# Shared expert tile moved to the end of the first expert pass, and a shorter start of the attention loop

## The reference

```
x = x + 0.5 * ffn(layernorm(x))      # first expert pass
x = x + attention(layernorm(x))      # 16 query heads, 4 key/value groups, head size 16, causal
x = x + 0.5 * ffn(layernorm(x))      # second expert pass, same weights
```

## Time and profile before

| | |
|---|---|
| median of 3 runs | 416.62 us (414.96 to 417.93) |
| profiled execution | 416.29 us, of which 414.5 us span |
| busy share | PE 90%, DVE 59%, ACT 35%, POOL 42% |
| first expert pass ends (last scatter issued) | 126.06 us |
| first scores of the loop | 170.67 us |
| step 3 of the loop | 185.66 us |
| last scatter of the second pass issued | 404.58 us |

### The profile page before, as it was taken

How to read it: one execution, slowest core, us unless ns; L and a number is a source line. 1 busy time by engine, 2 the same in 40 slices (tenths; PEclk the granted TensorE clock), 3 DMA queues, 4 the chain that set the end, 5 groups by cost and what they waited for, 6 DMA issues and landing times.

```text
span 414.5 us, 8450 instructions
## 1 busy us (share of the span) xinstructions
PE 374.9 (90%) x3164; PEld 294.5 (71%) x3171; DVE 243.0 (59%) x732; ACT 143.7 (35%) x296; POOL 175.3 (42%) x288
## 2 busy tenths in 40 slices
PE   8999999999998698888999999998699999999980
PEld 6769999999673455555566665555399999989660
DVE  5889852222222647778878778889757874222220
ACT  3221111111110234565767657577334111111110
POOL 1041425552111254556767664565812215643111
PEclk9999999999999979999999999999989999999996
DMA  8959932299103524202213042200211101398000
GB/s 266 409 207 351 333 106 76 66 334 333 40 16 114 156 81 126 56 20 78 78 48 105 20 121 71 55 28 28 59 57 37 43 25 56 103 345 318 27 23 14
DMA packets 27055, 50.04 MB, mean 121 GB/s; under 512 B 4458, under 2 KB 20590, under 8 KB 25975
## 3 DMA queue, kind: packets, MB, share of 16 engines
q1 hardware_dynamic: 19118, 25.10, 18.7%
q0 software_dynamic: 4512, 21.50, 15.1%
q10 hardware_dynamic: 3376, 2.80, 2.3%
HBM read 35.16 MB, written 6.55 MB: 101 GB/s over the span
## 4 chain that ended last, share of the span: by engine, by line
PE 67%; DVE 17%; DMA 5%; issue 4%; SPq 3%; ACT 1%; another core or an unknown queue 1%; POOL 1%; POOLq 0%; DVEq 0%; ACTq 0%
PE bank L1003 25%; PE bank L1024 13%; PE bank L1228 3%; PE bank L1457 3%; PE bank L1485 3%; PE bank L1386 2%; PE bank L542 2%; DVE mxa L1416 2%; PE bank L993 2%; PE bank L965 2%; PE bank L1514 2%; SPq L1333 1%; PE bank L1379 1%; DVE area L1534 1%; PE bank L592 1%
## 5 line engine op out<-in xcount | busy, mean ns | idle before, releaser
L1003 PEld LDWEIGHTS bank<-area,W 128*128 128x128 f32 x1024 | 119.9, 193 | 3.5 <-ACT area L1093 1.7
L1003 PE MATMUL bank<-area,W 128*128 128x128 f32 x1024 | 120.9, 277 | 1.2 <-ACT area L1093 1.2
L1172 DVE TENSOR_TENSOR area<-area,bank 128x512 f32<-128x512 f32 x34 | 23.4, 687 | 71.5 <-issue 49.7
L1464 ACT ACTIVATE area<-bank 128x512 f32<-128x512 f32 x96 | 54.2, 597 | 27.8 <-PE bank L1457 27.4
L1024 PE MATMUL bank<-W,area 128*128 128x256 f32 x256 | 60.9, 381 | 1.8 <-DVE area L1157 1.8
L1473 POOL TENSOR_SCALAR_AFFINE_SELECT area<-area 128x512 f32<-128x512 f32 x64 | 40.8, 650 | 40.5 <-ACT area L1464 40.2
L1104 ACT ACTIVATE area<-bank 128x512 f32<-128x512 f32 x34 | 20.3, 597 | 97.1 <-PE bank L1003 87.5
L1024 PEld LDWEIGHTS bank<-W,area 128*128 128x128 f32 x256 | 46.2, 190 | 7.9 <-issue 2.9
L1416 DVE TENSOR_REDUCE mxa<-bank 128x2 f32<-128x512 f32 x64 | 42.9, 673 | 7.2 <-PE bank L1388 7.1
L892 POOL DMA_INDIRECT out<-area,sidx x17 | 17.1, 1005 | 55.3 <-DVE area L1157 52.6
L892 POOL DMA_INDIRECT x2d<-area,sidx x17 | 17.1, 1006 | 54.7 <-DVE area L1157 54.7
(11 more groups left out here) (200 smaller groups left out, 574.3 us busy)
## 6 DMA issues: line engine op xcount, KB each, us to landing
W<-wall SPq DMA_DIRECT2D x24, 512.0 KB, 8.8
area<-area SPq DMA_DIRECT2D x48, 128.0 KB, 2.4
area<-x SPq DMA_DIRECT2D x8, 256.0 KB, 5.3
area<-x2d SPq DMA_DIRECT2D x8, 256.0 KB, 4.6
rows<-area ACTq DMA_DIRECT2D x8, 256.0 KB, 2.5
area<-JV SPq DMA_DIRECT2D x40, 32.0 KB, 1.9
cb<-constb ACTq DMA_DIRECT2D x1, 296.0 KB, 4.4
area<-x,gidx POOLq DMA_INDIRECT x18, 3.5
```

The lines of the kernel that those rows point to most:

```text
L1003: last = pe.matmul(ps[:, i * P:(i + 1) * P], W[:, w:w + P], xT[:, j % 2, c, :], start=(c == 0), stop=(c == C - 1))
L1172: v.tensor_tensor(out, sil[:, n % 2, :], bank[2 + n % 2][:], ALU.mult).then_inc(f_h[l], 1)
L1464: a.activation(PT[:, n % 2, u * 512:(u + 1) * 512], bank[u][:], ACT.Exp, scale=D ** -0.5).then_inc(a_e, 1)
```

## The change

- First pass only: the shared tile goes from position 15 to 16, the last. Its gate and up are issued in pieces, and the down product of position 15 comes between the first quarter and the rest. Its hidden values are transposed and copied behind the loop. The second pass keeps position 15, and its last down product goes to bank 7 and does not wait for `finish` of the position before.
- SP loads batch 0 of `x2d` once position 16's up product is made and the scatters of positions 0 to 15 have landed; batches 1 to 7 still wait for `s_fin`. DVE normalises batch 0 (`first_norm`) right behind its last `finish`.
- The statistics groups become batch 0, batch 1, batches 2 to 4 (before: 0, 1 to 3, 4); the last has its Newton steps on DVE. The shift instruction L393 (and L491 in the loop) is dropped, and the factor -0.5 does its work.
- Fillers ahead of the attention: 12 and, behind batch 0's projections, 20, in place of 48, 8, 3 and the single ones.
- Batch 0's row of maxima is negated, transposed and written in two halves (8 heads each), the first after two groups.
- The loop begins with 4 groups of maxima done, not 7. Steps 0, 1 and 2 make two groups each (4 and 5, 6 and 7, 8 and 9), later steps group n + 7 as before. Batch 1's row is copied in step 2 (before: step 1). Batch 3's transpose goes into step 0, and the last two split stages and two thirds of the stacks of batch 2 go behind the first exponentials.

```diff
-MIX = 15
+MIX = (2 * NE, 2 * NE - 1)
-WARM_MID = 48
+WARM_MID = 12
+WARM_NEXT = 20
...
-            link(nc.vector.tensor_scalar(hv[:, t0:t1], ve[:, t0:t1].bitcast(I32), 1, None,
-                                         ALU.arith_shift_right), seen)
-            nc.vector.tensor_scalar(rs[:, t0:t1], hv[:, t0:t1], -1.0, RSQRT_MAGIC,
+            nc.vector.tensor_scalar(rs[:, t0:t1], ve[:, t0:t1].bitcast(I32), -0.5, RSQRT_MAGIC,
...
+        def down_bank(l, n):
+            return bank[7] if l == 1 and n == NP - 1 else bank[6]
...
-            if n >= 1:
+            if n >= 1 and down_bank(l, n) is bank[6]:
                 pe.wait_ge(f_o[l], n)
...
+                    shared_gate_up(l, 0, (0,))
+                    if j == NP - 1:
+                        ffn_down(l, j - 1, offs[j - 1])
+                    shared_gate_up(l, 0, (1,))
+                    shared_gate_up(l, 1, (0, 1))
...
+        def first_norm(seen):
+            for t in range(*tiles(1, 0)):
+                ln_sums(1, t, seen)
+            ln_stats(1, 0, seen)
+            ln_newton(1, 0, seen, nc.vector)
+            ln_apply(0)
...
+        def maxima(n):
+            return (NG + 2 * n, NG + 2 * n + 1) if n < 3 else (n + NG + 3,)
...
-            sp.wait_ge(s_fin[0], 1)
+            sp.wait_ge(f_up[0], NP)
+            for i in range(OB):
+                sp.wait_ge(f_s[0][i], 16 * (2 * NE // OB))
             for b in range(B):
+                if b == 1:
+                    sp.wait_ge(s_fin[0], 1)
                 sp.dma_start(xt[:, TB * b:TB * b + TB, :],
...
```

Matrix engine, ahead of the loop and in it:

```diff
             a_proj_kv(0, PRO_KV[0])
+            warm(WARM_NEXT)
             ln_transpose(1, 1, PRO_T[1])
...
+            pe.wait_ge(s_one, 32)
+            pe.wait_ge(a_v, 2)
+            for u in range(3):
+                a_scores(0, u)
+            a_neg_pe(1)
...
+                if n == 0:
+                    pe.wait_ge(a_ms, 2)
+                    ln_transpose(1, 3, PRO_T[3])
...
                 a_values(n)
-                if m < NG * B:
+                if more:
                     a_small_masks(m)
                     a_max_pe(m, 2)
+                for x in own[1:]:
+                    a_max_pe(x, 0)
                 if g == 0 and b + 3 < B:
...
                     a_heads_pe(n - 1)
+                for x in own[1:]:
+                    a_max_pe(x, 1)
+                    a_max_pe(x, 2)
```

More of the change, by code:

```diff
@@ L178, in macaron @@
         ve = sb("ve", [P, NT])
-        hv = sb("hv", [P, NT], I32)
         rs = sb("rs", [P, NT], I32)
@@ L988, in ffn_gate_up @@
                 ps = bank[2 * m + j % 2]
[L989 to L996, removed]
+                if mixed(l, j):
+                    for c in range(C):
+                        w = (m * C + c) * I
                         last = pe.matmul(ps[:], xT[:, j % 2, c, :], W[:, bass.ds(off + w, I)],
                                          start=(c == 0), stop=(c == C - 1))
-                if not mixed(j):
+                else:
                     for i in range(IC):
@@ L1023, in ffn_down @@
                 else:
-                    last = pe.matmul(bank[6][:, 0:H], hT[:, n % 2, i, :],
-                                     W[:, bass.ds(off + at, H)] if mixed(n) else W[:, off + at:off + at + H],
+                    last = pe.matmul(ps[:, 0:H], hT[:, n % 2, i, :],
+                                     W[:, bass.ds(off + at, H)] if mixed(l, n) else W[:, off + at:off + at + H],
                                      start=(i == 0), stop=(i == IC - 1))
@@ L1053, in ffn_pe @@
             pe = nc.tensor
-            offs = [(tile_of(j) % NE) * WE for j in range(NP)]
+            offs = [(tile_of(l, j) % NE) * WE for j in range(NP)]
             for j in range(NP):
@@ L1163, in hidden @@
                 v.wait_ge(f_up[l], n + 1)
-                if not mixed(n):
+                if not mixed(l, n):
                     if n >= 2:
@@ L1197, in ffn_dve @@
                     normalise(l, j + 1)
+                if j == MIX[l] == NP - 1:
+                    finish(j - 1)
                 hidden(j)
@@ L1444, in a_scores @@
             r = b % QB
-            if g == 0 and u == 0:
-                pe.wait_ge(a_mq[r], 16 * (b // QB + 1))
+            if u == 0 and (g == 0 or n == NG // 2):
+                pe.wait_ge(a_mq[r], 16 if n == 0 else rows_sent(b))
             if n >= 1:
@@ L1631, in _ @@
             ln_evacuate(1, 0, PRO_T[0])
-            for b in range(2):
-                a_split_act(b, PRO_Q[b])
-                a_vt_act(b, PRO_KV[b])
-                a_split_act2(b)
-                a_stack_k(a, b, 0, slice(0, 2))
-                if b == 1:
-                    ln_evacuate(1, 2, PRO_T[2])
-                a_split_act3(b)
-                if b == 0:
-                    ln_evacuate(1, 1, PRO_T[1])
-                a_stack_k(a, b, 1)
+            a_split_act(0, PRO_Q[0])
+            a_split_act2(0)
+            a.wait_ge(s_fin[0], 1)
+            a_stack_k(a, 0, 0, slice(0, 1))
+            a_split_act3(0)
+            a_stack_k(a, 0, 1)
+            a_vt_act(0, PRO_KV[0])
+            a_stack_k(a, 0, 2)
+            ln_evacuate(1, 1, PRO_T[1])
+            a_split_act(1, PRO_Q[1])
+            a_split_act2(1)
+            a_stack_k(a, 1, 0, slice(0, 2))
+            a_vt_act(1, PRO_KV[1])
+            ln_evacuate(1, 2, PRO_T[2])
+            a_split_act3(1)
+            a_stack_k(a, 1, 1)
             a_split_act(2, PRO_Q[2])
@@ L1707, in _ @@
             ffn_dve(0, seen)
-            for t in range(*tiles(1, 0)):
-                ln_sums(1, t, seen)
-            ln_stats(1, 0, seen)
-            ln_newton(1, 0, seen, v)
-            ln_apply(0)
             for t in range(*tiles(1, 1)):
@@ L1765, in _ @@
                     a_max_dve(m, 2)
-                if g == 2 and b < B - 2:
-                    round_half(b, seen)
-                if g == 0 and b + 1 < B:
-                    a_neg_dve(b + 1)
+                if g == 0 and 1 <= b < B - 1:
+                    a_neg_dve(b + 2)
+                for x in own[1:]:
+                    for k in range(3):
+                        a_max_dve(x, k)
+                if n == 1:
+                    a_neg_dve(2)
                 if g == 0 and b + 5 < B:
@@ L1851, in _ @@
-                if m == NG - 1:
-                    pe.wait_ge(s_xs[1], 4)
-                    a_neg_pe(0)
-                if m == NG + 1:
-                    pe.wait_ge(s_one, 32)
-                    for u in range(3):
-                        a_scores(0, u)
+            pe.wait_ge(s_one, 32)
[3 more added lines that the diff above has]
+            a_neg_pe(1)
             for n in range(NG * B):
                 b, g = divmod(n, NG)
-                m = n + NG + 3
+                own = maxima(n)
+                m, more = own[0], m_left(n)
@@ L1908, in _ @@
                     a_heads_pe(n - 1)
+                for x in own[1:]:
+                    a_max_pe(x, 1)
+                    a_max_pe(x, 2)
                 if g == 3 and b + 4 < B:
-                    pe.wait_ge(a_ms, b + 2)
+                    pe.wait_ge(a_ms, b + 3)
                     if b >= 1:
```

256 lines of the change are left out of this document (141 added, 115 removed).

## The result

| | before | after |
|---|---|---|
| median of 10 runs | 417.69 us (414.96 to 420.10, and one of 548.04) | 414.15 us (410.00 to 415.71) |
| ratio, 95% interval | | 0.9889 (0.9859 to 0.9919) |
| profiled execution, span | 416.29, 414.5 us | 413.94, 412.1 us |
| first maxima on PE | 154.19 us | 150.06 us |
| first scores | 170.67 us | 163.27 us |

A forecast was written before the change was run, and what follows sets the result against it. Latencies were taken to bound the 45 us between first pass and first scores, PE and DVE nearly full in the loop. 416.29 - 8.0 (step 3) - 0.2 (later steps) - 0.65 (second pass) = 407.4 us; range 403 to 412.

The forecast's parts named there:

- the moved DMAs: SP's queue before the loop: batch 0's eight stack transfers run 135.2 to 140.2, land by 142.2, wanted at 143.5 us.
- the term of 8.0 us at step 3: Attention loop's step 3, from where both kernels' groups of maxima agree: 177.7 us, before 185.66, 8.0 us earlier.
- four rivals: Double steps cheaper (404, 0.15); clock falls (411.5, 0.12); early load not early (411.8, 0.06); half clock into loop (423, 0.04).
- End of first pass and early load: Between first pass and attention: new order costs 0.6 us; batch 0 normalised at 130.3 against 136.96, 6.7 us earlier.
- Batch 1 sets the pace: Ahead of the first maxima: batch 1, not batch 0, is the limit; its transpose at 139.3, before 144.27, 5.0 us earlier.
- rival 2: PE clock falls to half between 143 and 156 us, fillers among the maxima being gone: +4, 411.5 us; chance 0.12.
- No wait as long as 3 us: PE between 143 and 156 us: argument against a falling clock, that no PE wait there reaches 3 us.
- The rule of the Trainium skill that I weighed: PE clock: throttled is the default and activity releases it, so an idle array falls back to 1.2 GHz.
- First maxima to first scores: Ahead of the loop: DVE's twelve reductions take over as limit; first maxima at 143.5, first scores at 155.7 us.
- The loop pays back: Loop's first steps: step 3 comes 22 us behind first scores; three groups moved in cost 7 of the 15 us won.
- Bank 7: End of the second pass: last down product no longer waits for `finish`, 0.65 us saved.
- the forecast's chain: Start of attention: first maxima at 143.5, first scores at 155.7, step 3 at 177.7 us.

The follow-up runs named there:

- run 1: Changed kernel with the loads of batches 5 to 7 and both constant row transfers queued behind batch 0's stacks: 406.39 us, ratio 0.9777.
- run 2: Changed kernel with only the loads of batches 5 to 7 behind batch 0's stacks, constant rows ahead again: 409.14 us, ratio 0.9827.
- runs 5 and 6: Early load of batch 0 undone, in the changed kernel (416.69 us, ratio 0.9969) and in that of run 1 (417.96 us, ratio 1.0005).
- run 4: Changed kernel with 18 filler matmuls on PE ahead of the first maxima: 409.45 us, ratio 0.9863.
- run 10: Kernel before with only the second pass's last down product moved to bank 7: 413.60 us, ratio 0.9964.
- runs 2 and 7: Run 2, and the changed kernel with seven groups of maxima ahead of the loop, three behind the first scores: 410.61 us, ratio 0.9892.
- run 8: Run 1 with seven groups of maxima ahead of the loop and batch 1's row of maxima copied a step earlier: 409.19 us, ratio 0.9784.
- run 9: Run 8 with fillers moved to where PE idles (12 behind the last down product, one, then 27): 404.77 us, ratio 0.9754.

## Why the prediction was wrong

**The step that failed** is the sentence on the moved DMAs: "SP's eight stack transfers of batch 0 ... land by 142.2, and are wanted at 143.5". I took 2 us of landing, that of an empty queue, while the same paragraphs had moved the stacks from 3 us behind the loads' end into their middle. They were issued from 138.11 to 142.99, 3 us late, and the last landed at 150.0, 7.0 us behind its issue. The row I took the 0.6 us of issue from says nothing of a full queue, and I asked of each moved transfer when it is issued, not what is in flight then. A part of it could have been seen: seven loads of 256 KB, at the 290 GB/s or so which the windows of the kernel before show, take 6.3 us, and stacks issued from 135.2 meet them. That gives no 150.0: run 1's expectation, made by this sum, came out at half of the measured effect, and the constant rows, which the prediction does not price at all, have their part in the rest (run 2). In the sum it is the term of 8.0 us at step 3, which came out at -0.2 (185.66 before, 185.82 after). None of the four rivals was this one.

Point by point, predicted and measured (us; in the profiled execution the whole first pass, from its first gate product on, was 0.9 later, ahead of anything that the change touches):

| | predicted | measured |
|---|---|---|
| load of batch 0 issued | 123.3 | 123.67 |
| batch 0 normalised / transposed on PE | 130.3 / 130.4 | 131.15 / 133.29 |
| load of batch 1 issued | 130.6 | 132.4 |
| batch 1 transposed | 139.3 | 141.59 |
| batch 0's stacks landed | 142.2 | 150.0 |
| first maxima on PE | 143.5 | 150.06 |
| first maxima to first scores | 12.2 | 13.21 |
| first scores to step 3 | 22 | 22.55 |
| end of the second pass | -0.65 | -1.06 |

- *End of first pass and early load:* right in kind and, but for the shift, in size. The early load is worth more than the "6.7 us earlier" that I gave it, as the late one also meets a cold PE (runs 5 and 6).
- *Batch 1 sets the pace:* right, at 141.59, 2.3 late. The pass's last scatter took 4.2 us to land, not 3.42, and PE's fillers at half clock delayed batch 0 by 2.1 (some 0.7 of it at full clock too, by 0.219 us each).
- *Clock:* rival 2 had the right mechanism at 0.12, with the wrong cause. "No wait as long as 3 us" failed with the wait for the stacks. It happened twice, at 129.2 and at 149.7, and the second cost 2.7 us (run 4). The rule of the Trainium skill that I weighed (TensorE: Matmul & The Clock Gate, part 1, "What's actually happening") holds in this trace, at 0.50 in 153 to 154 behind four idle microseconds.
- *First maxima to first scores:* 13.21 for 12.2 is near by luck. The forecast had DVE as the limit; in the changed kernel the half clock was (10.5 us at full, run 4). Run 1, with no wait, took 12.81 with DVE as the limit, as forecast.
- *The loop pays back:* right. Predicted 22 to 22.5, measured 22.55. But I stopped the count at step 3. The step behind it took 3.49 us instead of 4.72, so 1.2 of what the double steps cost comes back.
- *Bank 7:* the mechanism right and the size near, 0.73 us for 0.65 (run 10); the end is another 0.33 us shorter, which is not explained.
- *With the collision gone* (run 1) the forecast's chain holds: first maxima 145.04, 12.81 to the first scores, 22.54 to step 3. Its ratio, 0.9777, is that of the forecast (407.4 of 416.62, 0.978), in part by luck, as its step 3 is still 2.7 us behind the forecast's 177.7.

The Trainium skill has the rule that I should have weighed (DMA: Bandwidth & Descriptors, "Queues, rings and completion order"): SP's DMAs all go over one row of rings, and an engine takes the descriptors of a ring in their order. By that rule a stack issued behind seven loads waits for what is left of them. The traces agree as far as that goes: 2.4 us of landing in an empty queue, 5.1 in the median and 7.0 at most behind the loads and the rows, 4.3 at most with three loads fewer ahead, 2.5 without the rows too. They also show what the rule doesn't give: loads ahead of the rows landed 3.4 us later at most with the rows behind them (7.7 against 4.3).

## What to carry to other kernels

A transfer that is moved earlier is priced by what is in flight on its queue at the new time, not by its landing time at the old one: list the bytes issued ahead of it. Order a queue by who waits first, and look at small transfers too: three loads and two row transfers that no one waited for yet cost the change half of its possible gain (ratio 0.9889 against 0.9777), and at the slowest stack the rows, 216 of 984 KB, made 1.8 of the 4.5 us. And where PE will wait in the new order, price the work behind the wait at half clock as well.

## What the runs showed that I had not expected

The clock fell behind idle stretches much shorter than the 3.08 us of the earlier trace rows, and not every time. With the same instructions, PE's 2.51 us (changed kernel, 126.7 to 129.2) were followed by 0.50, while in runs 2 and 7 idle stretches of 2.51 and 2.53 us at that place were followed by the full clock; behind a wait of about 2 us ahead of batch 1's transpose it fell in run 8 and not in run 1; in run 9 it fell behind 1.48 us. What decides between the two is not settled by these runs. It probably makes a part of the changed kernel's spread (410.0 to 415.7 us), and fillers in a fixed number don't cure it: when the clock is low they take 0.43 us each and delay what stands behind them.
